# The first attention of a fused transformer kernel: two key/value groups per pass, maxima carried in the queries' fourth slot, one bank for the weighted values of both, and a new order of work

## The chip, the cores and the metric

The kernel runs on one core of one Trainium2 chip. The metric is the time of one execution on the device in microseconds (us), the median of several runs.

## What is computed

The reference is two pre-norm transformer layers on x of 2 batches x 512 tokens x 512 features, in fp32: attention, feed-forward, attention, feed-forward, each added to x. The change touches the first attention. Its heads are small: 32 query heads of 16 features, 8 key/value groups, four query heads to a group.

```python
q, k = _apply_rope(q, cos, sin), _apply_rope(k, cos, sin)
k_h = jnp.repeat(k, GROUP_SIZE, axis=1)          # GROUP_SIZE = 4
scores = jnp.einsum('bhqd,bhkd->bhqk', q, k_h) / math.sqrt(HEAD_DIM)   # HEAD_DIM = 16
attn = jax.nn.softmax(where(causal, min, scores), axis=-1)
ctx = jnp.einsum('bhqk,bhkd->bhqd', attn, v_h)
return ctx.transpose(0, 2, 1, 3).reshape(b, t, D_OUT) @ Wo
```

## The kernel before, in words

TensorE multiplies fp32r operands, so each fp32 value is written as a high part (rounded to fp32r, by ScalarE) and a low part (the rest, by VectorE or GpSimd), and products are summed from such parts. The engines are PE (TensorE), DVE (VectorE), ACT (ScalarE), POOL (GpSimd) and SP (SyncE, which issues the loads).

`project0` (lines 867 to 1008) normalises eight tiles of 128 tokens, turns them, multiplies them with the joined weights and leaves three tensors in SBUF: `q2` and `k2`, four slots of 16 numbers for each head (queries high, low, high, low; keys high, high, low, low, so that 64 rows give all partial products), and `vw`, the values' high and low parts beside a column of ones for the softmax sum. DVE rotates (L984, L989, L990), POOL adds (L1004) and takes the keys' low part (L1007), DVE takes the queries' low part (L959). Before its statistics (L89) DVE sets the ones and zeros of `vw` (L963, L964).

`attend0` (from line 1011) goes over 16 units u, one for each group and batch, the batch changing fastest. A unit has four query tiles i, and tile i meets key tiles 0 to i, so a unit has 10 pairs (i, j), one per tick. The order is written as tables of ticks (`TURN`, `SCORE`, `SHIFT`, `END`, `BACK`) which every engine follows in its own queue. Per unit:

- `turn_qk` (L1117): PE transposes keys, then each query tile, four 64-column transposes at a time, into the one bank `qkbank`; ACT copies them (L1347) to `k_rows` and `q_rows`, which holds four query tiles.
- `scores` (L1129) with the mask (L1132): queries by keys into one of three score banks, 11 banks a unit; DVE takes the negated maxima (L1238).
- `part_maxima` (L1250, L1252) splits the four maxima of a tile into parts, `shift_maxima` (L1165) transposes them through the same `qkbank`, `spread_maxima` (L1260) writes them as eight more rows under the queries.
- `turned_scores` (L1145, mask L1148) computes keys by queries less the maximum, with 72 rows, into one of two banks; ACT takes the exponential (L1353) and its high part (L1359), POOL the low part (L1386).
- `weigh` (L1158, L1159) multiplies high and low parts with `vw`, 33 columns, into `cbank`. DVE reads the bank when a tile i is complete (L1270), `turn_back` (L1175) transposes it per head, and DVE adds the parts and divides by the sums (L1279, L1280, L1286, L1293).

The output projection takes each of eight token tiles when its heads are complete: `turn_tile` (L1203), high part (L1376), low part (L1315), twelve matmuls (`project_tile`, L1216 to L1218), the sum with x (L1329) and the statistics of the next norm (L1331). Because batches alternate, tile 0 comes only in the drain after the last unit and the other seven behind it. The next stage starts when the block has ended on every engine.

## Time and profile before

| | before |
|---|---|
| median of 3 runs | 1594.26 us (1590.72 to 1594.69) |
| profiled execution | 1589.34 us, its span 1587.5 us |
| PE busy, share of the span | 1488.5 us, 94% |
| DVE, ACT, POOL busy | 1080.5, 740.8, 692.0 us |
| mean granted TensorE clock | 0.964 |
| projection stage, from the trace | 0 to 74.5 us |
| first attention with its output projection | 74.5 to 441.0 us |

A matmul is pipelined, so its row is longer than its share of PE; where work follows without a gap, the distance between ends is its cost. PEld is the weight load, which may run beside a matmul. "Issue" is time in which the profile shows nothing that the engine waited for. The clock is in parts of 2.4 GHz; 0.50 is the level of 1.2 GHz.

### The profile page before, as it was taken

The page shows a single profiled execution, that of the slowest core. Times are in us where ns is not written, and L with a number is a line of the kernel's source. Part 1 is how long each engine was busy: PE and PEld are TensorE (multiplying, and loading weights), DVE is VectorE, ACT ScalarE, POOL GpSimd, SP SyncE. Part 2 cuts the span into 40 slices and gives each one's busy share as a digit, 9 for nine tenths or more (in the row PEclk, how much of TensorE's full clock was granted, in tenths as well). Part 3 has the DMA queues.
Part 4 walks back from the last instruction along what each step waited for, and adds up shares of the span by engine and source line. Part 5 has one row for each costly group of instructions (what it writes and reads, how often), then busy time and mean ns, then how long its engine had stood idle before and what let it go on. Part 6 is the DMA issues. An engine that isn't in the chain of part 4 may idle for free. (4 is left out here: it accounts for less than half of the span.)

```text
span 1587.5 us, 21452 instructions
## 1 busy us (share of the span) xinstructions
PE 1488.5 (94%) x7256; PEld 1090.3 (69%) x7256; DVE 1080.5 (68%) x2149; ACT 740.8 (47%) x1590; POOL 692.0 (44%) x528
## 2 busy tenths in 40 slices
PE   4699999999959988999999999999999999789999
PEld 3555555555624446888888888888888888668887
DVE  6678888888574345787777777777787677642322
ACT  3456666666332223445445455454444544443332
POOL 3556666666242324443434434243533334045453
PEclk9879999999869988999999999999999999999999
DMA  2000000000030001100100001010110101023332
GB/s 99 27 1 1 1 1 1 1 1 1 1 100 1 0 24 43 41 28 27 34 21 28 27 27 41 14 40 14 34 34 27 34 1 41 1 74 96 99 97 77
DMA packets 63669, 50.01 MB, mean 32 GB/s; under 512 B 7533, under 2 KB 52973, under 8 KB 63307
## 3 DMA queue, kind: packets, MB, share of 16 engines
q1 hardware_dynamic: 63563, 48.65, 10.5%
q8 instruction: 60, 0.98, 0.3%
q14 instruction: 46, 0.38, 0.1%
HBM read 46.54 MB, written 2.10 MB: 31 GB/s over the span
## 5 line engine op out<-in xcount | busy, mean ns | idle before, releaser
L1386 POOL TENSOR_TENSOR a_p_lo<-a_prob,a_p_hi 128x512 fp32r<-128x512 f32 x160 | 203.5, 1276 | 126.0 <-ACT a_p_hi L1359 124.5
L678 ACT ACTIVATE a_pt_hi<-a_ring 128x512 fp32r<-128x512 f32 x160 | 93.7, 596 | 176.2 <-PE a_ring L388 176.1
L814 POOL TENSOR_TENSOR a_rot_a<-a_rot_a,a_rot_b 128x512 f32<-128x512 f32 x80 | 103.3, 1292 | 148.5 <-DVE a_rot_b L557 147.6
L669 ACT ACTIVATE a_prob<-a_score,a_nmax 128x128 f32<-128x128 f32 (+3 forms) x256 | 131.9, 528 | 57.8 <-DVE a_nmax L522 57.7
L329 PE MATMUL a_xo<-h_hi,a_w_hi 128*128 128x512 f32 x384 | 155.3, 404 | 3.6 <-POOL a_w_lo L824 3.6
L1908 POOL TENSOR_TENSOR f_w_lo<-raw,f_w_hi 128x512 fp32r<-128x512 f32 (+2 forms) x66 | 90.9, 1401 | 142.8 <-ACT f_w_hi L1851 142.7
L331 PE MATMUL a_xo<-h_hi,a_w_lo 128*128 128x512 f32 x384 | 152.0, 396 | 0.0
L330 PE MATMUL a_xo<-h_lo,a_w_hi 128*128 128x512 f32 x384 | 150.9, 393 | 0.0
L1353 ACT ACTIVATE a_prob<-a_turned 128x512 f32<-128x512 f32 x160 | 94.9, 593 | 94.5 <-PE a_turned L1145 53.0
L819 POOL TENSOR_TENSOR a_p_lo<-a_rot_a,a_p_hi 128x512 fp32r<-128x512 f32 x80 | 103.8, 1297 | 72.0 <-ACT a_p_hi L695 72.0
L539 DVE TENSOR_TENSOR a_pt_lo<-a_ring,a_pt_hi 128x512 fp32r<-128x512 f32 x160 | 108.5, 686 | 33.3 <-ACT a_pt_hi L678 32.1
L1238 DVE TENSOR_REDUCE a_nmax<-a_score 128x1 f32<-128x384 f32 (+3 forms) x176 | 109.0, 640 | 30.8 <-PE a_score L1132 30.3
L522 DVE TENSOR_REDUCE a_nmax<-a_score 128x1 f32<-128x384 f32 (+3 forms) x176 | 109.3, 636 | 17.0 <-PE a_score L378 12.0
L824 POOL TENSOR_TENSOR a_w_lo<-raw,a_w_hi 128x512 fp32r<-128x512 f32 x48 | 63.4, 1325 | 105.3 <-ACT a_w_hi L706 104.3
L533 DVE TENSOR_SCALAR a_prob<-a_prob,a_rinv 128x128 f32<-128x128 f32 (+3 forms) x256 | 105.9, 456 | 4.6
L329 PE MATMUL a_xo<-a_wo_hi,a_c_hi 128*128 128x512 f32 x256 | 104.5, 408 | 1.5 <-DVE a_c_lo L544 1.4
L695 ACT ACTIVATE a_p_hi<-a_rot_a 128x512 fp32r<-128x512 f32 x80 | 50.4, 630 | 109.6 <-POOL a_rot_a L814 109.6
L1359 ACT ACTIVATE a_p_hi<-a_prob 128x512 fp32r<-128x512 f32 x160 | 100.3, 627 | 2.7
L331 PE MATMUL a_xo<-a_wo_hi,a_c_lo 128*128 128x512 f32 x256 | 100.3, 392 | 0.0
L330 PE MATMUL a_xo<-a_wo_lo,a_c_hi 128*128 128x512 f32 x256 | 100.1, 391 | 0.0
L329 PE MATMUL a_score<-a_p_hi 128*128 128x128 f32 (+3 forms) x256 | 93.9, 367 | 5.2 <-POOL a_p_lo L819 4.6
L829 POOL TENSOR_TENSOR a_wo_lo<-raw,a_wo_hi 128x512 fp32r<-128x512 f32 x32 | 42.1, 1326 | 124.1 <-ACT a_wo_hi L714 124.1
(273 smaller groups left out, 3938.3 us busy)
## 6 DMA issues: line engine op xcount, KB each, us to landing
raw<-in_L_gate_up_t SPq DMA_DIRECT2D x40, 256.0 KB, 3.0
raw<-in_L_attn_wq SPq DMA_DIRECT2D x32, 256.0 KB, 2.8
raw<-in_L_attn_wo SPq DMA_DIRECT2D x32, 256.0 KB, 2.6
raw<-in_L_down_t SPq DMA_DIRECT2D x20, 256.0 KB, 2.7
x<-in_L_attn_x SPq DMA_DIRECT2D x4, 512.0 KB, 5.2
raw<-in_L_attn_wk SPq DMA_DIRECT2D x8, 256.0 KB, 2.7
raw<-in_L_attn_wv SPq DMA_DIRECT2D x8, 256.0 KB, 2.7
out<-x SPq DMA_DIRECT2D x8, 256.0 KB, 2.5
```

The lines of the kernel that those rows point to most:

```text
L329: nc.tensor.matmul(out, l_hi, r_hi, start=start, stop=False)
L330: nc.tensor.matmul(out, l_hi, r_lo, start=False, stop=False)
L331: return nc.tensor.matmul(out, l_lo, r_hi, start=False, stop=stop)
L522: nc.vector.tensor_reduce(nmax[:, i % 2, bank * per:(bank + 1) * per], score[e % NS][:, 0:per * n].rearrange("p (h n) -> p h n", h=per), A ...
L533: last = nc.vector.tensor_scalar(pr, pr, rinv[:, i % 2, h:h + 1], None, ALU.mult)
L539: nc.vector.tensor_tensor(pt_lo[:, n % NPT, :], ring[n % 2][:, :], pt_hi[:, n % NPT, :].bitcast(F32), ALU.subtract).then_inc(ring_read, 1)
L669: nc.scalar.activation(prob[i % 2][:, h, 0:n], score[e % NS][:, (h % per) * n:(h % per + 1) * n], ACT.Exp, bias=nmax[:, i % 2, h:h + 1], a ...
L814: nc.gpsimd.tensor_tensor(rot_a[:, c % 2, :], rot_a[:, c % 2, :], rot_b[:, c % 2, :], ALU.add).then_inc(summed, 1)
L819: nc.gpsimd.tensor_tensor(p_lo[:, u % 2, c, :], rot_a[:, c % 2, :], p_hi[:, u % 2, c, :].bitcast(F32), ALU.subtract).then_inc(p_ready, 1)
L1238: nc.vector.tensor_reduce(nmax[:, i, bank * per:(bank + 1) * per], score[e % NS][:, 0:per * n].rearrange("p (h n) -> p h n", h=per), AX_X, ...
L1359: nc.scalar.activation(p_hi[:, mm % NP, :], prob[:, mm % NE, :], ACT.Copy).then_inc(p_hi_done, 1)
L1386: nc.gpsimd.tensor_tensor(p_lo[:, mm % NP, :], prob[:, mm % NE, :], p_hi[:, mm % NP, :].bitcast(F32), ALU.subtract).then_inc(p_ready, 1)
```

## The change

A pass now takes a pair of groups of one batch: 8 passes, batch 0 first. Queries and keys of both groups are transposed together with all 128 columns; `k_rows` holds each group's keys with zeros in the other group's 64 rows. The fourth slot of each key is 1 and that of each query 0; once the maxima of a query tile are known, their two parts are put into that slot and the four transposes are done again (`turn_queries` with `again`), and DVE copies the result to `q_max`. The low x low product is left out of the scores. `q_rows` holds one query tile. The weights of both groups give 66 rows of one bank. Tiles, waits and engines follow a new order written out by hand, of which PE's is shown; `first` is the first of two output tiles of batch 0 in the second and third pass of batch 1, `tail` the pass after the last. DVE copies the keys and the second transposes, ACT the first ones. `c_own` is no longer loaded, and the weights' columns are laid out anew on the host.

```diff
     def tokens(self, t):
-        return slice((self.first + t) * P, (self.first + t + 1) * P)
+        at = (self.first + t) % self.wrap
+        return slice(at * P, (at + 1) * P)
...
-                nc.scalar.activation(m.vw[:, t, :, :, 0:HD0], twice(kvbank[t % 2][:, KW:2 * KW]), ACT.Copy).then_inc(read, 1)
+                v = kvbank[t % 2][:, KW:2 * KW].rearrange("p (g x n) -> p g x n", x=2, n=HD0)
+                nc.scalar.activation(m.vw[:, t, :, 1, 0:3:2, 0:HD0], v, ACT.Copy)
+                nc.scalar.activation(m.vw[:, t, :, 0, 0:3:2, 0:HD0], v, ACT.Copy).then_inc(read, 1)
...
-                nc.vector.tensor_tensor(m.q2[:, t, :, 1:4:2, :], twice(rot_a[:, t % 2, 0:QW]),
-                                        m.q2[:, t, :, 0:4:2, :].bitcast(F32), ALU.subtract).then_inc(q_ready, 1)
+                nc.vector.tensor_tensor(m.q2[:, t, :, 1, :], rot_a[:, t % 2, 0:QW].rearrange("p (h n) -> p h n", n=HD0),
+                                        m.q2[:, t, :, 0, :].bitcast(F32), ALU.subtract).then_inc(q_ready, 1)
 
             for t in range(NT):
-                nc.vector.memset(m.vw[:, t, :, :, HD0:HD0 + 1].bitcast(F32), 1.0)
-            nc.vector.memset(m.vw[:, :, :, 1, HD0 + 1:2 * HD0 + 1].bitcast(F32), 0.0).then_inc(v_ready, 1)
+                nc.vector.memset(m.vw[:, t, :, :, 0:3:2, HD0].bitcast(F32), 1.0)
+                nc.vector.memset(m.vw[:, t, :, 1, 0:3:2, HD0 + 1:2 * HD0 + 1].bitcast(F32), 0.0)
+            nc.vector.memset(m.q2[:, :, :, 3, :].bitcast(F32), 0.0).then_inc(v_ready, 1)
             ln.scales(dve)
...
+            nc.gpsimd.memset(m.k2[:, :, :, 3, :].bitcast(F32), 1.0)
+            nc.gpsimd.memset(m.vw[:, :, :, :, 1, :].bitcast(F32), 0.0)
...
-                nc.gpsimd.tensor_tensor(m.k2[:, t, :, 2:4, :], twice(rot_a[:, t % 2, QW:QW + KW]),
-                                        m.k2[:, t, :, 0:2, :].bitcast(F32), ALU.subtract).then_inc(k_ready, 1)
+                nc.gpsimd.tensor_tensor(m.k2[:, t, :, 2, :], rot_a[:, t % 2, QW:QW + KW].rearrange("p (g n) -> p g n", n=HD0),
+                                        m.k2[:, t, :, 0, :].bitcast(F32), ALU.subtract).then_inc(k_ready, 1)
...
+        k_rows = sb("k_rows", [P, 2, X2, T], F32R)
+        q_rows, q_max = sb("q_rows", [P, HPG, P], F32R), sb("q_max", [P, NQ, HPG, P], F32R)
+        nmax = sb("nmax", [P, 2, HPG, X2])
...
+            def claim_qkbank(reader, value):
+
+                if emptied:
+                    pe.wait_ge(*emptied.pop())
+                emptied.append((reader, value))
+
+            def claim_score():
+
+                count["score"] += 1
+                if count["score"] > NS:
+                    pe.wait_ge(score_read, count["score"] - NS)
+                return score[(count["score"] - 1) % NS]
+
...
+            def turn_queries(u, i, again):
+
+                if not live(u):
+                    return
+                b, p, n = u // PAIRS, u % PAIRS, QT * u + i
+                if again:
+                    pe.wait_ge(parted, 2 * (n + 1))
+                    claim_qkbank(qm_read, n + 1)
+                else:
+                    claim_qkbank(q_read, n + 1)
+                for r in range(HPG):
+                    at = X2 * (HPG * p + r)
+                    x = m.q2[:, b * QT + i, at:at + X2, :, :].bitcast(F32)
+                    last = nc.tensor.transpose(qkbank[:, r * P:(r + 1) * P], x.rearrange("p x s n -> p (x s n)"), m.ident[:, :])
+                last.then_inc(qm_turned if again else q_turned, 1)
...
+                if x == 0 and bank == 0:
+                    pe.wait_ge(q_read, QT * u + i + 1)
...
+                    nc.tensor.matmul(out[:, h * n:(h + 1) * n], q_rows[:, bank * per + h, :], k_rows[:, u % 2, x, 0:n],
+                                     start=(h == 0), stop=False)
...
+                last = nc.tensor.matmul(out, k_rows[:, u % 2, x, j * P:(j + 1) * P], q_max[:, (QT * u + i) % NQ, :, :],
...
+                v = m.vw[:, (u // PAIRS) * QT + j, u % PAIRS, :, x:x + 2, :].rearrange("p s c n -> p s (c n)")
+                nc.tensor.matmul(cbank[0:VX, :], v[:, 0, :], p_hi[:, mm % NP, :], start=first, stop=False)
+                nc.tensor.matmul(cbank[0:VX, :], v[:, 1, :], p_lo[:, mm % NP, :], start=False,
+                                 stop=last).then_inc(weighed, 1)
...
+                    last = nc.tensor.transpose(hbank[:, h * VX:(h + 1) * VX], head_t[0:VX, n % 2, h * P:(h + 1) * P],
+                                               m.ident[0:VX, 0:VX])
...
+            for u in range(-1, NU + 1):
+                turn_queries(u - 1, 3, 1)
+                weigh(u - 1, 1, 1, 1)
+                turned_scores(u - 1, 2, 0, 2)
+                turned_scores(u - 1, 2, 1, 2)
+                turn_keys(u)
+                weigh(u - 1, 2, 0, 0)
+                turn_back(u - 1, 1)
+                turned_scores(u - 1, 3, 0, 0)
+                weigh(u - 1, 2, 1, 0)
+                weigh(u - 1, 2, 0, 1)
+                if tail:
+                    turn_tile(QT)
+                scores(u, 0, 0, 0)
+                turn_queries(u, 1, 0)
+                scores(u, 0, 1, 0)
+                weigh(u - 1, 2, 1, 1)
+                turned_scores(u - 1, 3, 1, 0)
+                turned_scores(u - 1, 3, 0, 1)
+                scores(u, 1, 0, 0)
+                weigh(u - 1, 2, 0, 2)
+                weigh(u - 1, 2, 1, 2)
+                turned_scores(u - 1, 3, 1, 1)
+                turn_queries(u, 0, 1)
+                turned_scores(u - 1, 3, 0, 2)
+                if tail:
+                    project_tile(QT)
+                    turn_tile(QT + 1)
+                scores(u, 1, 0, 1)
+                scores(u, 1, 1, 0)
+                scores(u, 1, 1, 1)
+                turn_queries(u, 2, 0)
+                if first is not None:
+                    turn_tile(first)
+                weigh(u - 1, 3, 0, 0)
+                weigh(u - 1, 3, 1, 0)
+                turned_scores(u - 1, 3, 1, 2)
+                scores(u, 2, 0, 0)
+                turned_scores(u - 1, 3, 0, 3)
+                scores(u, 2, 0, 1)
+                scores(u, 2, 0, 2)
+                turn_back(u - 1, 2)
+                scores(u, 2, 0, 3)
+                scores(u, 2, 1, 0)
+                turn_queries(u, 1, 1)
+                weigh(u - 1, 3, 0, 1)
+                turned_scores(u - 1, 3, 1, 3)
+                if tail:
+                    project_tile(QT + 1)
+                turned_scores(u, 0, 0, 0)
+                weigh(u - 1, 3, 1, 1)
+                scores(u, 2, 1, 1)
+                scores(u, 2, 1, 2)
+                turn_queries(u, 3, 0)
+                scores(u, 2, 1, 3)
+                if first is not None:
+                    project_tile(first)
+                    turn_tile(first + 1)
+                weigh(u - 1, 3, 0, 2)
+                turned_scores(u, 0, 1, 0)
+                scores(u, 3, 0, 0)
+                scores(u, 3, 0, 1)
+                scores(u, 3, 0, 2)
+                weigh(u - 1, 3, 1, 2)
+                if tail:
+                    turn_tile(QT + 2)
+                weigh(u - 1, 3, 0, 3)
+                turned_scores(u, 1, 0, 0)
+                scores(u, 3, 0, 3)
+                turned_scores(u, 1, 1, 0)
+                weigh(u - 1, 3, 1, 3)
+                if tail:
+                    project_tile(QT + 2)
+                turn_queries(u, 2, 1)
+                turned_scores(u, 1, 0, 1)
+                scores(u, 3, 1, 0)
+                weigh(u, 0, 0, 0)
+                turn_back(u - 1, 3)
+                scores(u, 3, 1, 1)
+                turned_scores(u, 1, 1, 1)
+                weigh(u, 0, 1, 0)
+                turn_queries(u + 1, 0, 0)
+                turned_scores(u, 2, 0, 0)
+                scores(u, 3, 1, 2)
+                scores(u, 3, 1, 3)
+                if first is not None:
+                    project_tile(first + 1)
+                weigh(u, 1, 0, 0)
+                turned_scores(u, 2, 1, 0)
+                weigh(u, 1, 1, 0)
+                weigh(u, 1, 0, 1)
+                turn_back(u, 0)
+                turned_scores(u, 2, 0, 1)
+                turned_scores(u, 2, 1, 1)
...
+            def put_maxima(u, i):
+
+                if not live(u):
+                    return
+                n, t, at = QT * u + i, (u // PAIRS) * QT + i, X2 * HPG * (u % PAIRS)
+                heads = m.q2[:, t, at:at + X2 * HPG, 3, :]
+                both = nmax[:, i % 2, :, :].rearrange("p h x -> p (h x)")
+                dve.wait_ge(score_read, count["score"])
+                nc.vector.tensor_copy(heads[:, :, 0], both).then_inc(parted, 1)
+                dve.wait_ge(parted, 2 * n + 1)
+                nc.vector.tensor_tensor(heads[:, :, 1], both, heads[:, :, 0].bitcast(F32), ALU.subtract).then_inc(parted, 1)
+
...
+                nc.vector.tensor_copy(k_rows[0:64, u % 2, 0, :], qkbank[0:64, :]).then_inc(keys_read, 1)
+                nc.vector.tensor_copy(k_rows[64:P, u % 2, 1, :], qkbank[64:P, :]).then_inc(keys_read, 1)
+
+            def read_queries(u, i):
...
+                dve.wait_ge(qm_turned, n + 1)
+                if n >= NQ:
+                    s = n - NQ
+                    dve.wait_ge(t_scored, weight_at(s // QT, s % QT, 1, s % QT) + 1)
+                nc.vector.tensor_copy(q_max[:, n % NQ, :, :], qkbank[:, :].rearrange("p (h n) -> p h n", h=HPG)).then_inc(qm_read, 1)
...
+            def read_queries(u, i):
+                if not live(u):
+                    return
+                n = QT * u + i
+                act.wait_ge(q_turned, n + 1)
+                if n >= 1:
+                    act.wait_ge(scored, scored_by(n - 1))
+                nc.scalar.activation(q_rows[:, :, :], qkbank[:, :].rearrange("p (h n) -> p h n", h=HPG),
+                                     ACT.Copy).then_inc(q_read, 1)
...
-                    m.h_hi, m.h_lo = isb("h0_hi", [P, KT, NT * P], F32R), isb("h0_lo", [P, KT, NT * P], F32R)
+                    m.h_hi, m.h_lo = isb("h0_hi", [P, KT, QT * P], F32R), isb("h0_lo", [P, KT, QT * P], F32R)
...
-    out["L0_qkv"] = np.concatenate([a["L0_attn_Wq"], a["L0_attn_Wk"], a["L0_attn_Wv"]], axis=1)
+    wq = a["L0_attn_Wq"].reshape(D, NG // 2, 2, HPG, HD0).transpose(0, 1, 3, 2, 4).reshape(D, -1)
+    out["L0_qkv"] = np.concatenate([wq, a["L0_attn_Wk"], a["L0_attn_Wv"]], axis=1)
```

## Rows read from the trace of the kernel before

**Rows 1.** Busy time by stretch: us, each engine (instructions), clock, DMA share, GB/s
```profile
74.50:88.00 13.50, 12.10 (x42) 6.79 (x42) 5.17 (x12) 3.97 (x6) 0.94 (x1) 0.50 0.24 79
88.00:108.00 20.00, 18.15 (x73) 9.58 (x71) 14.83 (x26) 14.03 (x27) 14.88 (x12) 0.75 0.00 0
128.00:399.00 271.00, 261.08 (x1371) 145.39 (x1370) 230.96 (x589) 189.12 (x340) 174.17 (x138) 1.00 0.00 1
399.00:411.20 12.20, 11.49 (x37) 5.14 (x38) 5.74 (x16) 6.14 (x10) 7.34 (x6) 0.61 0.00 1
411.20:441.00 29.80, 27.14 (x133) 21.66 (x131) 17.25 (x29) 4.69 (x8) 0.00 (x0) 0.99 0.00 1
```

**Rows 2.** Waits of TensorE's weight loads, 239 to 399 us: total, times, longest
```profile
PEld a_turned L1145 <- DVE a_q_rows L1260: 7.9, 8, 1.0
PEld a_qkbank L1165 <- DVE a_split L1252: 6.8, 9, 0.8
```

**Rows 3.** Key transposes: timeline row of one group, then the line's first and last start
```profile
216.88 0.60 PE L1117 MATMUL a_qkbank<-ident,k 128*64 128x128 f32 x4
...
L1117 PE MATMUL a_qkbank<-ident,k x64: 270/272/421, 74.5 to 376.0; 128*64 128x128 f32 x64
```

**Rows 4.** Timeline (start, us, engine, line): transposes at 205, output tiles at 420
```profile
204.87 0.39 PE L1145 MATMUL a_turned<-a_q_rows,a_k_rows 72*128 72x512 f32 x1
205.10 0.60 PE L1117 MATMUL a_qkbank<-ident,q 128*64 128x128 f32 x4
205.63 0.43 PE L1175 MATMUL a_hbank<-ident,a_head_t 33*128 33x33 f32 x4
205.79 0.58 ACT L1347 ACTIVATE a_q_rows<-a_qkbank 64x512 fp32r<-64x512 f32 x1
...
419.95 0.39 PE L1218 MATMUL a_score<-a_wo_hi,a_c_lo 128*128 128x512 f32 x1
420.18 0.60 PE L1203 MATMUL a_turned<-ident,a_head 128*128 128x128 f32 x4
420.51 0.19 PEld L1216 LDWEIGHTS a_score<-a_wo_hi,a_c_hi 128*128 128x128 f32 x1
423.42 0.60 PE L1203 MATMUL a_turned<-ident,a_head 128*128 128x128 f32 x4
```

**Rows 5.** Groups by line and form, 239 to 399 us
```profile
L1386 POOL TENSOR_TENSOR a_p_lo<-a_prob,a_p_hi 128x512 fp32r<-128x512 f32 x82 | 104.3, 1276 | 57.1 <-ACT a_p_hi L1359 56.3
L1359 ACT ACTIVATE a_p_hi<-a_prob 128x512 fp32r<-128x512 f32 x81 | 50.8, 627 | 1.3
L1353 ACT ACTIVATE a_prob<-a_turned 128x512 f32<-128x512 f32 x81 | 48.1, 593 | 46.9 <-PE a_turned L1145 26.4 <-PE a_turned L1148 20.0
L1347 ACT ACTIVATE a_q_rows<-a_qkbank 64x512 fp32r<-64x512 f32 x32 | 18.5, 579 | 0.0
L1270 DVE COPY a_head_t<-a_cbank 33x512 f32<-33x512 f32 x33 | 22.2, 673 | 0.1
L1145 PEld LDWEIGHTS a_turned<-a_q_rows,a_k_rows 72*128 72x128 f32 x81 | 15.7, 194 | 14.9 <-DVE a_q_rows L1260 7.9
L1117 PEld LDWEIGHTS a_qkbank<-ident,q 128*64 128x64 f32 x124 | 13.7, 110 | 4.1
L1165 PEld LDWEIGHTS a_qkbank<-ident,a_split 128*128 128x128 f32 x33 | 4.6, 140 | 9.7 <-DVE a_split L1252 6.8
```

**Rows 6.** Projection stage: timeline rows, then L1004 with its min/median/max ns
```profile
5.47 0.91 DVE L964 MEMSET vw<- 128x1024 f32 x1 [0.15 <-issue]
9.34 2.63 DVE L89 BATCH_NORM_STATS2 stats<-x 128x6 f32<-128x512 f32 x4 [0.24 <-DMA x<-in_L_attn_x]
...
42.16 1.21 DVE L959 TENSOR_TENSOR q<-p_rot_a,q 128x1024 fp32r<-128x1024 f32 x1
...
L1004 POOL TENSOR_TENSOR p_rot_a<-p_rot_a,p_rot_b x8: 1522/2461/2482, 31.4 to 69.4; 128x640 f32<-128x640 f32 x8
```

More of the change, by code:

```diff
@@ L1122, in scores @@
[L1122 to L1127 removed]
+            count = {"score": 0}
+            emptied = []
+            def claim_qkbank(reader, value):
+                if emptied:
+                    pe.wait_ge(*emptied.pop())
+                emptied.append((reader, value))
@@ new lines, in project_tile @@
+                    high = nc.tensor.matmul(out[:, :], c_hi[:, t % 2, k, :], wo_lo[:, k, :], start=False, stop=False)
+                    last = nc.tensor.matmul(out[:, :], c_lo[:, t % 2, k, :], wo_hi[:, k, :], start=False, stop=(k == KT - 1))
+                high.then_inc(projected, 1)
+                last.then_inc(scored, 1)
+            for u in range(-1, NU + 1):
+                first = 2 * (u - PAIRS - 1) if u in (PAIRS + 1, PAIRS + 2) else None
+                tail = u == NU
+                turn_queries(u - 1, 3, 1)
[91 more added lines that the diff above has]
+                turned_scores(u, 2, 1, 1)
@@ L1379, in _ @@
         @block.gpsimd
         def _(pool):
-            nc.gpsimd.memset(k_rows[S64, :, :].bitcast(F32), 1.0).then_inc(ones_set, 1)
-            for mm in range(TICKS * 2 * NG):
+            for mm in range(M_ALL * NU):
                 pool.wait_ge(p_hi_done, mm + 1)
```

492 lines of the change are left out of this document (253 added, 239 removed).

## The prediction

> **What bounds the kernel now.** I read the stretches by stage first, because the change touches only the first projection and the first attention, some 440 of 1587.5 us. In [rows 1] TensorE (PE) is busy in 261.08 of 271.00 us of the attention's even part (96%) at a granted clock of 1.00; VectorE (DVE) has 85%, ScalarE (ACT) 70%, GpSimd (POOL) 64%. So PE sets the pace there, and the question for every edit is what it does to PE's queue. The same rows show where PE is slow for another reason: from 74.50 to 88.00 the clock is 0.50 (the 1.2 GHz level) though PE is busy in 12.10 of 13.50 us, from 88.00 to 108.00 it is 0.75, and from 399.00 to 411.20, where the last weights drain, 0.61.
>
> The second view is what PE waited for in eight units [rows 2]: its weight loads stood 7.9 us for the spread maxima (L1260) and 6.8 us for the split maxima (L1252), the only waits of size on another engine. Part of each lies under a matmul that still runs: PE as a whole idles 9.92 us in the 13.6 units of the even part [rows 1].
>
> The third is the pace. Key transposes of one unit begin at 216.88, and those of the last, eight units on, have their last start at 376.0 [rows 3], some 0.3 us into their group of four: (376.0 - 0.3 - 216.88)/8 = 19.9 us per unit, 39.8 per pair of units. The stage takes 441.0 - 74.5 = 366.5 us. Of these 16 x 19.9 = 318.4 are units; output tiles follow each other at 423.42 - 420.18 = 3.24 us [rows 3, 4], eight are 25.9; the remaining 22.2 are the low clock (half of 24 us at the head, 12; 0.39 of 12.2 us at the drain, 5) and some 5 of filling and draining.
>
> **The change, part by part, per pair of units.** PE's work goes by ends: where work follows without a gap, an instruction costs the distance from the end before to its own.
> - Transposes. Before, a pair has 10 groups of four 64-column ones (keys and queries), 8 single ones of the split maxima and 8 groups of turn-back. After it has 9 groups of four 128-column ones (keys 1, queries 4, queries with maxima 4) and 4 turn-backs of 66 rows. Four of 64 columns end 205.70 (205.10 + 0.60) behind a matmul that ended 205.26: 0.44 us. Four of 128 columns end 420.78 behind 420.34: 0.44. Four turn-backs end 206.06 behind 205.70: 0.36 [rows 4]. A split transpose I put at 0.11, a quarter of the four. Before: 10 x 0.44 + 8 x 0.11 + 8 x 0.36 = 8.2. After: 9 x 0.44 + 4 x 0.40 (the wider output, between 0.36 and 0.44) = 5.6. Removed: 2.6 us.
> - Scores, turned scores, masks and weighings keep their count and free size (22, 20, 8 and 40 per pair). The stationary operand grows in rows (64 or 72 to 128) and for the weighing in columns (33 to 66). The first I cost at nothing: 72 rows load in 0.19 [rows 5] and 128 rows in 0.19 (L1216, [rows 4]). The weighing's load grows only to 66 columns, under that 0.19 of 128, and both lie beneath the 0.23 from one 512-wide matmul's start to the next start (419.95 to 420.18, [rows 4]).
> - Waits removed. The spread from a PSUM slot (L1260) and the split bank go; 9.92 us of idle over 6.8 pairs is 1.5 per pair, the loads' 14.7 over four pairs 3.7. I take 2.2, which is also what 39.8 leaves over the sum of PE's own pieces by ends.
> - Waits added. The queries' buffer is now one instead of four: ACT may copy tile i's queries only when every score of tile i-1 is done, and PE's next scores wait for that copy. This happens four times per pair. In three of them PE has two to four instructions of 0.23 in between, some 0.94 us, and the copy takes 0.58 [rows 5] plus two handovers of about 0.1 (transposes end 205.70, the copy began 205.79, [rows 4]): 0.8. It fits if ACT is free. ACT is a queue of exponentials and high parts of 0.59 and 0.63 us [rows 5], and is 20 x 1.22 + 4 x 0.58 = 26.7 us busy per pair, so it is often in one of them: half of 0.6 late on average. All nine claims of the shared bank (before: 18) and the maxima's second way (a DVE copy as long as L1270's 0.67 [rows 5], with about 2.5 us of PE work in between) add to that. I take 1.7, with bounds 0 and 6.8 (below).
> - Other engines. DVE has 230.96 of 271.00 us [rows 1], 33.9 per 39.8. It loses eight spreads, four head reads and four head takings per pair and gains six copies of 0.67 at most, so it stays below that. POOL keeps 20 x 1.276 = 25.5 [rows 5]. Neither reaches PE's 37.
>
> Sum per pair: -2.6 - 2.2 + 1.7 = -3.1, so 36.7 us, eight of them 293.6, against 318.4.
>
> **Order of the output tiles.** Batch 0 is now complete after half the pairs, and its four tiles go into two middle passes, the other four into the drain. The PE work stays 25.9; it lies beside nothing before and fills gaps of at most a few tenths after. At the drain one chain remains without cover: the last weighing, head read 0.67, turn-back, head taking, tile transposes, high and low part, 2.8 of projection, add and statistics; I add 2 us for it. The stage: 293.6 + 25.9 + 22.2 + 2 = 343.7, or -22.8.
>
> **Projection stage.** DVE now clears the fourth slots of all queries before the statistics: 4096 elements at 0.91 per 1024 [rows 6] is 3.6 us, with eight small memsets about 4.3 less the 0.9 removed. The second four statistics waited only 0.24 us for their data, at 9.34 [rows 6], so DVE has no slack there and nearly all of it, 3.3 us, moves the start of everything. Bounds: 2 (memset faster) and 5. Against it, the low part of the queries halves from 1024 to 512 elements, 1.21 to about 0.68 (a 512-element copy has 0.67). It lies beside POOL's sum of 2.46, whose shortest is 1.52 [rows 6]; a shorter neighbour should give 0.45 back in six tiles, 2.7, and the last low parts end the stage 1 us sooner. ACT's second write of the values is short and fits in its idle time. POOL's new memsets (3136 elements) come while it would wait for the first weights to land. Net -0.4, with bounds -4 and +5. Behind the stage nothing changes.
>
> Sum: -23.2 us. The profiled execution took 1589.34 us (span 1587.5); the median of the three runs is 1594.26, 4.9 above it (0.3%, about what can be told from no change here). On the median: 1571.1, so 1571.
>
> **A rule against it.** The rows give 0.44 for four narrow and for four wide transposes [rows 4]. The Trainium skill ("TensorE: Matmul & The Clock Gate", section "LDWEIGHTS (loading the stationary operand)") says the load time is the number of columns over 1.2 GHz. By it a wide load is 53 ns longer than a narrow one; 36 of them exposed would, as an estimate, take 1.9 us per pair, 15 us in all, from the gain. The same section says that rows don't matter, and there the loads of 72 and 128 rows agree.
>
> **Rivals.**
> 1. The waits vanish (added wait 0): -4.8 per pair, -38.4, with +2 and -0.4: 1557. For it: PE's order keeps work between each producer and consumer. Against: one buffer where there were four. Chance 0.2.
> 2. The wide loads are exposed, or the clock stays low. By rows, 128 columns load in 0.140 and 64 in 0.110 [rows 5]: 36 x 0.03 is 1.1 per pair, 8.6 in all: 1580. The first pass has scores and transposes alone, about 21 us of full-clock work; if the 1.2 GHz level holds through it and through the drain, another 10 to 18 us go: 1581 to 1589. Chance together 0.17. The rule of the Trainium skill above stands beside the first half; by its figure that would be 1586.
> 3. Slower: the copy of the queries becomes the bound. Place: ACT's `read_queries` between two groups of scores. If the exponential queued before it waits for POOL's 1.276 us (three slots of `prob`), each of four copies comes 1.28 + 0.8 + 0.6 after the last score, with 0.94 covered: 1.7, or 6.8 per pair instead of 1.7. Then a pair takes 41.8, +2.0, and the whole +16 - 0.4 + 2: 1612. It decides from an added wait of 4.6 per pair, 1.15 per copy. For it: ACT at 73% in a fixed order. Against: the order puts each copy where its scores should be done. Chance 0.1.
> 4. The change doesn't do what it says, the pace stays 19.9 per unit because PE's modelled work hides a floor elsewhere: 1594 +-4. Chance 0.05.
>
> **Numbers.** The forecast has 0.48; its own range, added waits 0.7 to 2.7 and the start's bounds, is 1562 to 1582. The range takes in rival 1 and most of rival 2: 1550 to 1592. Faster by over 0.3% (below 1589.5): 0.48 + 0.2 + 0.14 = 0.82; same: 0.03 + 0.05 = 0.08; slower: 0.10.
>
> **What would show it.** Key transposes of two units following each other in the even part 36.7 us apart (35 to 38); PE at 96% or more there and its waits now on the copy of queries (ACT) and the second copy (DVE), under 0.3 us each; four wide transposes in 0.44; no L1252 or L1260 left; first statistics near 10 instead of 6.5 us; half clock for about as long at the head. I am wrong if a pair takes over 39.5 us with waits on ACT's copy, if the first pass runs over 35 us, or if the stretch before the first key transposes grows by more than 5 us.

## The result, and the profile after

| | before | after |
|---|---|---|
| median of 4 runs, us | 1592.49 (1588.54 to 1594.69) | 1519.81 (1516.26 to 1523.64) |
| ratio | 1 | 0.9547 [0.9508, 0.9585] |
| profiled execution, us | 1589.34 | 1516.26 |
| its span, us | 1587.5 | 1514.5 |

The change takes 72.7 us off the median. The forecast took off 23 and its range ended at 1550, so the forecast was wrong: right in sign, three times too small.

The first fence is the head of the page of after, busy time and share of each engine over the span. The second is the view of busy time by stretch (columns as in [rows 1]).

```profile
span 1514.5 us, 20230 instructions
...
PE 1411.0 (93%) x7032; PEld 1074.7 (71%) x7032; DVE 1009.6 (67%) x1918; ACT 711.5 (47%) x1550; POOL 689.4 (46%) x529
```

```profile
72.00:90.00 18.00, 14.33 (x59) 10.92 (x58) 11.01 (x20) 3.07 (x4) 0.00 (x0) 0.51 0.19 58
90.00:110.00 20.00, 14.25 (x73) 8.09 (x73) 13.64 (x25) 14.12 (x26) 15.10 (x13) 1.00 0.00 1
130.00:230.00 100.00, 98.75 (x586) 65.48 (x584) 90.25 (x189) 83.18 (x151) 86.74 (x69) 1.00 0.00 1
...
234.00:271.00 37.00, 34.25 (x191) 23.19 (x190) 28.70 (x59) 24.73 (x45) 23.25 (x20) 1.00 0.00 1
360.00:371.00 11.00, 7.62 (x34) 5.35 (x34) 4.97 (x11) 0.60 (x1) 0.00 (x0) 1.00 0.00 0
```

In the even part PE is busy 98.75 of 100 us, where [rows 1] has 261.08 of 271.00. The shares, 98.75% and 96%, hardly differ, yet the pace does. A group of key transposes now opens a pass over two units (timeline rows: start, duration, engine, line):

```profile
73.54 1.11 PE L1106 MATMUL a_qkbank<-ident,k 128*128 128x128 f32 x4 [0.69 <-ACT a_q_rows L1468]
...
140.76 0.66 PE L1106 MATMUL a_qkbank<-ident,k 128*128 128x128 f32 x4
...
170.29 0.66 PE L1106 MATMUL a_qkbank<-ident,k 128*128 128x128 f32 x4
...
229.40 0.66 PE L1106 MATMUL a_qkbank<-ident,k 128*128 128x128 f32 x4
```

A pair of units takes (229.40 - 140.76)/3 = 29.55 us (29.6 below), against 39.8 before [rows 3] and 36.7 in the forecast. All eight passes begin at 73.54, 109.89, 140.76, 170.29, 199.84, 229.4, 268.65 and 308.18: the first takes 36.35 (half clock up to 90, some 16 us of it), the two that carry two output tiles each 39.2 and 39.5.

What held PE back in the even part, first the weight loads and then PE as a whole (columns as in [rows 2], 130 to 230 us):

```profile
PEld a_score L1140 <- issue: 7.3, 35, 0.3
PEld a_turned L1156 <- issue: 5.6, 24, 0.3
PEld a_qkbank L1122 <- DVE q L1334: 2.9, 4, 0.7
PEld a_qkbank L1106 <- DVE a_q_max L1356: 0.8, 4, 0.2
PEld a_score L1137 <- ACT a_q_rows L1468: 0.8, 3, 0.3
```

```profile
PE a_qkbank L1122 <- DVE q L1334: 1.2, 4, 0.3
```

The waits for the split and spread maxima, 14.7 us in four pairs in [rows 2], are gone. In their place stands 1.2 us in 3.4 pairs, at the second transposition of the queries (L1122, for the low part of the maxima, L1334). The copy of the queries (L1468), the centre of the forecast's added waits, delays loads by 0.8 us in all.

The first attention stage now runs from 71.7 to 371.6, 299.9 us against 366.5; the stage before it ends 2.8 earlier. In the projection stage (timeline rows):

```profile
6.73 3.47 DVE L968 MEMSET q<- 128x4096 f32 x1 [0.80 <-issue]
10.12 4.78 DVE L89 BATCH_NORM_STATS2 stats<-x 128x6 f32<-128x512 f32 x8
```

and, by line and form, 20 to 74 us:

```profile
L1010 POOL TENSOR_TENSOR p_rot_a<-p_rot_a,p_rot_b 128x640 f32<-128x640 f32 x8 | 15.5, 1935 | 13.4 <-DVE p_rot_b L994 13.4
...
L962 DVE TENSOR_TENSOR q<-p_rot_a,q 128x512 fp32r<-128x512 f32 x8 | 5.7, 715 | 2.8 <-ACT k L933 2.8
```

### The profile page after: what moved, and what is told of

Read it like the earlier page. It is cut to its first block and busy times, and to the rows that moved or that the text cites. A ratio compares the mean times of both kernels' runs of the same rounds, so it can differ in the third digit from the quotient of the medians.

```text
span 1514.5 us, 20230 instructions
## 1 busy us (share of the span) xinstructions
PE 1411.0 (93%) x7032; PEld 1074.7 (71%) x7032; DVE 1009.6 (67%) x1918; ACT 711.5 (47%) x1550; POOL 689.4 (46%) x529
## 5 line engine op out<-in xcount | busy, mean ns | idle before, releaser
L523 DVE TENSOR_REDUCE a_nmax<-a_score 128x1 f32<-128x384 f32 (+3 forms) x176 | 109.3, 636 | 17.3 <-PE a_score L379 12.2
L1320 DVE TENSOR_REDUCE a_nmax<-a_score 128x1 f32<-128x512 f32 (+3 forms) x176 | 105.1, 635 | 20.2 <-PE a_score L1140 20.1
L534 DVE TENSOR_SCALAR a_prob<-a_prob,a_rinv 128x128 f32<-128x128 f32 (+3 forms) x256 | 99.2, 430 | 4.5
```

The lines of the kernel that those rows point to most:

```text
L523: nc.vector.tensor_reduce(nmax[:, i % 2, bank * per:(bank + 1) * per], score[e % NS][:, 0:per * n].rearrange("p (h n) -> p h n", h=per), A ...
L534: last = nc.vector.tensor_scalar(pr, pr, rinv[:, i % 2, h:h + 1], None, ALU.mult)
L1320: nc.vector.tensor_reduce(nmax[:, i % 2, bank * per:(bank + 1) * per, x], next_score()[:, 0:per * n].rearrange("p (h n) -> p h n", h=per), ...
```

## The experiments

A pair is 7.1 us shorter than forecast, and added waits that did not come are only 1.3 of it. The rest lies in what I took for PE's own work, or in waits that the kernel before had. Two theories stood against each other. **R, rows:** a stationary operand of 64 rows among operands of 128 costs something that does not show as the duration of its load. **O, order:** the old order with the maxima's way through DVE (split, transposed, spread) has a floor of its own, which my 2.2 us of removed waits undercounted. I began from before and made its operands full one after another, then went back from after. Times with their before are medians measured on the same chip; "pace" is the distance between key transposes in the trace, per unit (before 19.9) or per pair.

**Control.** Before, with the keys copied into two slots by the same ACT instruction (one for each kind of scores), and two buffers sharing space to make room.

```diff
-        k_rows = sb("k_rows", [P, B, T], F32R)
+        k_rows = sb("k_rows", [P, B, 2, T], F32R)
```

> Control for the next kernel: the kernel before, with the keys copied by ACT into two slots of k_rows at once (one write of 1024 instead of 512 elements per unit) and the output weights kept in the not yet used half of head. All products and their row counts are as before. Every theory: the unit keeps its 19.9 us within 0.2, the whole is within 5 us of the kernel before.

Measured: 1601.08, one run, 14 above the median of before on that chip and 2.2 above the slowest of its 15 runs (1579.39 to 1598.86), so the expected 5 us were missed. The trace shows one place: from 90 to 126 us the clock was 0.50 to 0.58, where before had 0.78 to 0.91 in the same stretch. In the even part the pace is 20.12 against 19.85, so the control brings nothing by itself; 0.3 us per unit are lost.

**Scores over 72 rows** instead of 64, eight of them zero in the keys' slot; the products are the same.

```diff
-                    nc.tensor.matmul(out[:, h * n:(h + 1) * n], q_rows[0:64, i, bank * per + h, :],
-                                     k_rows[0:64, u % 2, 0, 0:n], start=(h == 0), stop=False)
+                    nc.tensor.matmul(out[:, h * n:(h + 1) * n], q_rows[0:S64.stop, i, bank * per + h, :],
+                                     k_rows[0:S64.stop, u % 2, 0, 0:n], start=(h == 0), stop=False)
```

> The control with one edit: the scores' matmuls contract over 72 rows (eight of them zero) instead of 64. Theory R (rows: a stationary operand of at most 64 rows between operands of 128 rows is not loaded under the matmul before it, so each score and each mask behind it pays its load in the open): a score bank of 512 with its mask falls from 0.57 to about 0.36 us, as after the change; 11 banks give 2.0 to 2.5 us per unit, 16 units 32 to 40 us, so about 1552 to 1562 us, less if another engine's wait comes up. Rival O (order: the loss was waits that the old order of ticks forced, and rows cost nothing): a unit stays at 19.9 and the whole at 1590 +- 5.

Measured: 1575.04 against 1587.07, 0.9926 [0.9892, 0.9959]; pace 19.13. Its timeline at one full-width score, and what its loads waited for from 130 to 330 us:

```profile
213.42 0.19 PEld L1131 LDWEIGHTS a_score<-a_k_rows,a_q_rows 72*128 72x128 f32 x1
213.45 0.48 PE L1131 MATMUL a_score<-a_k_rows,a_q_rows 72*128 72x512 f32 x1
213.77 0.10 PEld L1134 LDWEIGHTS a_score<-mask_b,ident_b 128*128 128x128 bf16 x1 [0.15 <-issue]
```

```profile
PEld a_qkbank L1167 <- DVE a_split L1254: 15.9, 32, 1.0
PEld a_turned L1147 <- DVE a_q_rows L1262: 14.4, 21, 0.8
```

Two scores of full width in a row, with the mask between them, first here and then in before, where they have 64 rows:

```profile
228.34 0.51 PE L1131 MATMUL a_score<-a_k_rows,a_q_rows 72*128 72x512 f32 x1
228.69 0.23 PE L1134 MATMUL a_score<-mask_b,ident_b 128*128 128x128 bf16 x1
228.73 0.48 PE L1131 MATMUL a_score<-a_k_rows,a_q_rows 72*128 72x512 f32 x1
```

```profile
212.78 0.48 PE L1129 MATMUL a_score<-a_k_rows,a_q_rows 64*128 64x512 f32 x1
213.19 0.23 PE L1132 MATMUL a_score<-mask_b,ident_b 128*128 128x128 bf16 x1
213.35 0.18 PEld L1129 LDWEIGHTS a_score<-a_k_rows,a_q_rows 64*128 64x128 f32 x1
213.35 0.50 PE L1129 MATMUL a_score<-a_k_rows,a_q_rows 64*128 64x512 f32 x1
```

The second score begins 0.39 us behind the first, in before 0.57. The difference has two parts: from a score's start to its mask's are 0.32 to 0.35 us instead of 0.41, and from the mask's start to the next score's 0.04 instead of 0.16. So both loads come late in before, that of the 64-row score and that of the 128-row mask behind it. More rows for PE, and it is faster: R is at work. But a unit gave only 1.0 of the 2 to 2.5 that 11 banks at 0.2 promise, and the time lies above the expected 1552 to 1562. The view of waits in the control has 9.3 and 8.2 for the split and the spread maxima, where this one has 15.9 and 14.4. What PE saved, it mostly waited for the maxima.

**And the turn-back over 66 rows** (33 of them zero), on top of the last:

```diff
-                    last = nc.tensor.transpose(hbank[:, h * VW:(h + 1) * VW], head_t[0:VW, n % 2, h * P:(h + 1) * P],
-                                               m.ident[0:VW, 0:VW])
+                    last = nc.tensor.transpose(hbank[:, h * VB:(h + 1) * VB], head_t[0:VB, n % 2, h * P:(h + 1) * P],
+                                               m.ident[0:VB, 0:VB])
```

> The kernel before with scores of 72 rows and turn-backs of 66 rows instead of 33 (the added rows are zeros). Theory R: four turn-backs fall from 0.36 to about 0.25 us and what stands behind them loads early again, so 0.4 to 0.8 us per unit below the kernel with scores of 72 rows alone, 6 to 13 us in all. Rival O: no difference from the kernel before, or slightly longer for the wider output.

Measured: 1573.11, 0.9922 [0.9897, 0.9947]; pace 19.13. By ends, four turn-backs fall from the 0.36 of [rows 4] to 0.25, and the unit does not become shorter, where 0.4 to 0.8 us were expected.

**And everything wide**: the weighing with 66 columns instead of 33, key and query transposes with 128 instead of 64 (the neighbour's columns go along, unused).

```diff
-                nc.tensor.matmul(cbank[0:VW, :], v[:, 0, :], p_hi[:, mm % NP, :], start=(j == 0), stop=False)
+                nc.tensor.matmul(cbank[0:2 * VW, :], m.vw_flat[:, at:at + 2 * VW], p_hi[:, mm % NP, :], start=(j == 0), stop=False)
...
-                        x = m.q2[:, b * QT + s - 1, HPG * g + r, :, :]
+                        x = m.q2_all[:, b * QT + s - 1, HPG * g + r:HPG * g + r + 2, :, :]
```

> The kernel before with nothing below 65 rows or columns on the array: scores of 72 rows, turn-backs of 66, weighings of 66 columns and transposes of queries and keys of 128 columns (the extra columns are a neighbour's and not read). Order, passes and engines stay. Theory R alone: what remains to the new kernel is 2.6 us of transposes per pair, so a unit of about 16 to 17 us and the whole near 1535 to 1545. Theory R with O (both count): the unit stops at 17.3 to 18 us with waits on the maxima's way. Rival O alone: 1590 +- 5.

Measured: 1568.72, 0.9902 [0.9867, 0.9937]; pace 19.13 a third time. Waits of its loads, and its row of busy time by stretch:

```profile
PEld a_qkbank L1172 <- DVE a_split L1259: 17.3, 21, 1.2
PEld a_turned L1152 <- DVE a_q_rows L1267: 16.0, 21, 1.0
```

```profile
130.00:330.00 200.00, 178.39 (x1056) 112.92 (x1056) 180.09 (x449) 149.77 (x262) 132.92 (x106) 1.00 0.00 1
```

Three kernels with different work for PE and one pace: in the old order something other than PE's work holds the unit at 19.13. I had expected 16 to 18 with R, with or without O.

What columns cost can't be read from this pace, since something else holds it; the ends show it. Weighings with 66 columns follow each other 0.23 us apart in after (starts 188.45, 188.68, 188.91), those with 33 columns 0.24 in before (214.66, 214.90). Four transposes of 128 columns end 0.43 behind the matmul before them (after with 64-row turned scores: 199.79 and 199.36), four of 64 columns 0.44 [rows 4]. PE's busy time in 200 us is 178.39 here and 177.60 in the kernel before this one. So columns cost next to nothing, neither 33 to 66 nor 64 to 128, which answers the first half of rival 2. By the Trainium skill ("TensorE: Matmul & The Clock Gate", section "LDWEIGHTS (loading the stationary operand)") each load grows with its columns; the load rows do, from 110 to 140 ns for 64 and 128 columns [rows 5], by 30 ns and not by the 53 that the page's rule gives as an estimate. The distances between ends don't grow.

**The other way round: after, with scores over 64 rows.** Each group's scores contract only its own half of the rows; the other half is zero, so the sums are the same.

```diff
-                    nc.tensor.matmul(out[:, h * n:(h + 1) * n], q_rows[:, bank * per + h, :], k_rows[:, u % 2, x, 0:n],
+                    nc.tensor.matmul(out[:, h * n:(h + 1) * n], q_rows[64 * x:64 * x + 64, bank * per + h, :], k_rows[64 * x:64 * x + 64, u % 2, x, 0:n],
```

> The changed kernel with the scores contracted over the 64 rows of their own group (0 to 63 or 64 to 127) instead of over 128, half of which are zero: the same sums. Theory R (a stationary operand of 64 rows beside one of 128 loads in the open): 22 banks and their masks lose about what b1 won, 0.1 to 0.2 us each, so a pair of groups goes from 29.6 to 32 to 34 us and the whole by 20 to 35 us, to 1540 to 1555. Rival O (rows cost nothing): 29.6 and 1520 +- 5; two row halves might even run beside each other and save a little.

Measured: 1562.73 against 1588.91, 0.9859 [0.9815, 0.9904]; pairs begin at 151.63, 186.88 and 222.08, 35.2 apart: +5.6 per pair of 22 banks, 0.25 each, more than the expected 0.1 to 0.2 (a pair of 32 to 34, 1540 to 1555 in all). Timeline of this kernel:

```profile
198.45 0.40 PE L1153 MATMUL a_turned<-a_q_max,a_k_rows 128*128 128x512 f32 x1
198.78 0.18 PEld L1137 LDWEIGHTS a_score<-a_k_rows,a_q_rows 64*128 64x128 f32 x1 [0.36 <-issue]
198.78 0.44 PE L1137 MATMUL a_score<-a_k_rows,a_q_rows 64*128 64x384 f32 x1
199.15 0.10 PEld L1140 LDWEIGHTS a_score<-mask_b,ident_b 128*128 128x128 bf16 x1 [0.18 <-issue]
199.15 0.23 PE L1140 MATMUL a_score<-mask_b,ident_b 128*128 128x128 bf16 x1
```

and of after, scores of full width:

```profile
187.46 0.48 PE L1137 MATMUL a_score<-a_k_rows,a_q_rows 128*128 128x512 f32 x1
...
187.78 0.10 PEld L1140 LDWEIGHTS a_score<-mask_b,ident_b 128*128 128x128 bf16 x1 [0.15 <-issue]
187.78 0.23 PE L1140 MATMUL a_score<-mask_b,ident_b 128*128 128x128 bf16 x1
187.79 0.20 PEld L1137 LDWEIGHTS a_score<-a_k_rows,a_q_rows 128*128 128x128 f32 x1
187.82 0.48 PE L1137 MATMUL a_score<-a_k_rows,a_q_rows 128*128 128x512 f32 x1
```

In after the next score's load begins at 187.79, 0.22 us before the mask's row ends (188.01), and bank follows bank in 187.82 - 187.46 = 0.36 us. With 64 rows the load begins at 198.78, only 0.07 before the row of the turned score ahead of it ends (198.85), after 0.36 us of idle. The mask behind shows the same: its load begins 0.07 before the end of the 64-row score (199.15 and 199.22), but 0.16 before that of the 128-row score (187.78 and 187.94). The loads' own durations are alike, 0.18 and 0.20: not the load is dearer, its place is.

**After, with turned scores over 64 rows**, the same edit at the other product:

```diff
-                last = nc.tensor.matmul(out, k_rows[:, u % 2, x, j * P:(j + 1) * P], q_max[:, (QT * u + i) % NQ, :, :],
+                last = nc.tensor.matmul(out, k_rows[64 * x:64 * x + 64, u % 2, x, j * P:(j + 1) * P], q_max[64 * x:64 * x + 64, (QT * u + i) % NQ, :, :],
```

> The changed kernel with the turned scores (20 matmuls of 512 columns per pair) contracted over the 64 rows of their own group instead of 128: the same sums. Theory R: each stands between operands of 128 rows, so about 0.15 to 0.2 us per matmul and as much for what follows: a pair goes from 29.6 to 32 to 34 us, the whole to 1540 to 1555. Rival O: 29.6 and 1520 +- 5.

Measured: 1548.5, 0.9763 [0.9729, 0.9796]; pair 33.83, +4.3 for 20 matmuls, 0.21 each. One of them, in the timeline:

```profile
197.75 0.50 PE L1137 MATMUL a_score<-a_k_rows,a_q_rows 128*128 128x512 f32 x1
...
198.09 0.23 PE L1140 MATMUL a_score<-mask_b,ident_b 128*128 128x128 bf16 x1
198.24 0.18 PEld L1153 LDWEIGHTS a_turned<-a_q_max,a_k_rows 64*128 64x128 f32 x1
198.25 0.50 PE L1153 MATMUL a_turned<-a_q_max,a_k_rows 64*128 64x512 f32 x1
```

The matmul before it is the mask, whose row ends at 198.32; the load begins 0.08 before that, where the 128-row load above began 0.22 before the end of such a mask. Before had 72 rows here [rows 4], so this price was never paid before the change; it is a second measurement of the same effect.

**What holds the old order at 19.13.** From the all-wide kernel, the spread of the maxima writes one head's columns instead of four:

```diff
-                nc.vector.tensor_tensor(q_rows[S64, i, :, :],
+                nc.vector.tensor_tensor(q_rows[S64, i, 0:1, :],
```

> The kernel before with nothing below 65 rows or columns (unit 19.13 us), and the spread of the maxima writes one head's columns instead of four; it leaves out the maxima of three heads. Theory D (what held the unit at 19.13 in three kernels with different PE work is DVE's queue with the maxima's way in it: split, transpose, spread): 4 spreads shorter by about 0.4 us, unit 17.4 to 18.2. Rival P (PE's own instructions are the 19.13): unit stays at 19.1.

Measured: 1557.48 (one run), pace 18.08, 1.05 less, in the band of the theory that DVE's queue with the maxima's way in it holds the unit.

The same, and the head read copies 128 of 512 columns:

```diff
-                nc.vector.tensor_copy(head_t[0:VW, n % 2, :], cbank[0:VW, :])
+                nc.vector.tensor_copy(head_t[0:VW, n % 2, 0:P], cbank[0:VW, 0:P])
```

> The same, and the copy of the weighted values reads 128 of 512 columns; it leaves out the maxima and the results of three heads of four. Theory D with the whole queue as the bound: another 0.27 to 0.4 us for each of 4 copies, unit down to 16.9 to 17.3, where PE's own work ends it. Theory D with only the maxima's way as the bound: no further fall. Rival P: 19.1.

Measured: 1545.62 (one run), pace 17.70, only 0.38 less, between the two bands expected. DVE's busy time fell by 1.2 and then 1.3 us per unit (from the stretch rows), so its total alone is not the bound; the length of the maxima's way was the better candidate. The next one tests it.

**The all-wide kernel without the maxima's way.** The maxima are taken and not used: no split, no transposed split, no spread, and PE waits for none of them.

```diff
-    SHIFT = {6: (1, 0), 8: (1, 1), 9: (1, 2), 3: (0, 3)}
+    SHIFT = {}
...
-                if j == 0:
-                    pe.wait_ge(max_rows, QT * u + i + 1)
```

> The kernel before with nothing below 65 rows or columns (unit 19.13 us) and the maxima taken but not used: no split, no transpose of the split, no spread, so the exponentials are taken without subtracting the maximum and nothing on PE waits for DVE's maxima. PE loses 4 single transposes per unit, 0.45 us. If the maxima's way through DVE is what held that kernel: the unit falls to what PE's own work is, 15.5 to 16.5 us. If other waits of the old order (bank of the weighted values, copies by ACT) hold as much: 17 to 18.5. If PE's instructions themselves are the 19.13: 18.7.

Measured: 1521.75 (one run). Key transposes, and the busy row:

```profile
220.94 0.60 PE L1122 MATMUL a_qkbank<-ident,k 128*128 128x128 f32 x4
...
236.91 0.60 PE L1122 MATMUL a_qkbank<-ident,k 128*128 128x128 f32 x4
```

```profile
130.00:330.00 200.00, 194.62 (x1222) 133.69 (x1221) 168.97 (x390) 174.70 (x314) 159.66 (x126) 1.00 0.00 1
```

The pace is 15.97, in the band that says the maxima's way held it: 19.13 - 15.97 = 3.2 us per unit. Four split transposes at 0.11 are work left out; the other 2.7, 5.4 per pair, was waiting, direct or behind it. This takes away DVE's splits and spreads together with the waits (DVE is busy 3.7 us less per unit, and PE's wait for its head read is gone too, 6.1 us in 200 in the all-wide kernel), so it shows what the way costs as a whole, not which link of it.

This kernel's pair of 31.9 us can be compared with after's 29.6, since neither has 64-row operands nor the long way. One more group of transposes and four more turn-backs make 0.44 + 4 x 0.25 = 1.4 of the difference, the idle time that is left (5.4 us in 200 here, 1.25 in 100 there) 0.5; 0.5 is unassigned.

**After once more**, as the partner of the next two:

> The changed kernel once more, on the chip of the next two: 1520 +- 5 us, a ratio of 0.955 to the kernel before.

Measured: 1518.61 against 1589.16, 0.9555 [0.9527, 0.9583]. Its seventh pass begins at 265.56 where the first trace has 268.65, and yet both stages end at 371.6. The 3.1 us are lost in the drain, where the clock was 0.79 from 352 to 360 us and 0.75 from 366 to 372; in the first trace it was 1.00 from 308 us on. Behind the stage the code is the same in every kernel here, and that part took between 1139 and 1148 us in the fourteen traces.

**After, with the fourth slots of the queries cleared by POOL** instead of DVE:

```diff
-            nc.vector.memset(m.q2[:, :, :, 3, :].bitcast(F32), 0.0).then_inc(v_ready, 1)
...
             nc.gpsimd.memset(m.vw[:, :, :, :, 1, :].bitcast(F32), 0.0)
+            nc.gpsimd.memset(m.q2[:, :, :, 3, :].bitcast(F32), 0.0)
```

> The changed kernel with the zeros of the queries' fourth slots (4096 elements per partition) written by POOL, idle then, instead of DVE ahead of its statistics. If the 3.47 us memset delays everything behind it: statistics begin near 6.5 instead of 10.1 us and end near 12 instead of 14.9, and the first key transposes come 2 to 3 us earlier, the whole 2 to 3 us shorter. Rival (the start is paced by the weights' parts on POOL, which now also has the memset): 0 +- 1.

Measured: 1518.18, 0.9557 [0.953, 0.9583], the same as after. In the trace the first key transposes come at 70.79 instead of 73.29, 2.5 sooner, POOL taking 3.52 us for it. The stage ends at 370.0, only 1.6 sooner: the second pass took 30.81 us against 29.25, with a clock of 0.54 to 0.61 from 106 to 110 us. The median shows 0.4 of it. That is the rival's 0 +- 1, but not for the rival's reason, since the start did move.

**And the first output tile's transposes two weighings and a turned score later** in PE's order:

```diff
-                if first is not None:
-                    turn_tile(first)
                 weigh(u - 1, 3, 0, 0)
                 weigh(u - 1, 3, 1, 0)
                 turned_scores(u - 1, 3, 1, 2)
+                if first is not None:
+                    turn_tile(first)
```

> The same, and in the two passes with output tiles of batch 0 the first tile's transposes come three steps later, behind two weighings and a turned score, so that they no longer wait for ACT's copy of the queries right before them. If that wait (0.8 us, twice) is what makes these passes 39.2 instead of 29.6 + 6.5 us: each 0.8 to 1.5 us shorter, 2 to 3 in all. Rival (the loss is the shared bank, held by the tile until its low part is read): 0 to 0.5 each.

Measured: 1514.04 (1513.21 to 1515.97), 0.9529 [0.9505, 0.9554]: the lowest time of all, 4.6 under after on the same chip (1518.61), though the two ratios' intervals overlap. The passes with tiles take 38.3 and 38.6 instead of 39.3 and 39.6, 2.0 us together, in the expected band; the rest of the 4.6 is not shown to come from this edit.

## Why the prediction was wrong

**The step that failed** is in the change part by part: "The stationary operand grows in rows (64 or 72 to 128) ... The first I cost at nothing: 72 rows load in 0.19 [rows 5] and 128 rows in 0.19 (L1216, [rows 4])." Both durations are right, and beside the point. A score's 64-row load begins only about 0.07 us before the matmul ahead of it ends, a 72- or 128-row one 0.2 and more before, and the mask's load behind a 64-row score is late as well. The price was in the trace: two scores of full width of before begin 0.57 us apart (212.78 and 213.35, mask between them, shown above), which I took for what a score and its mask cost, and carried over. After has 0.36. With 64 rows put back, after loses 5.6 us per pair. I had also compared only 72 with 128 rows; the one form that mattered, 64, was missing from the comparison. And I had allowed this step no gain, so the range had nothing for it.

The Trainium skill ("TensorE: Matmul & The Clock Gate", section "LDWEIGHTS (loading the stationary operand)") says rows don't matter, and for a load's duration the trace agrees (0.18 to 0.20 us). The same page, section "Step-by-step: what each phase is for", has a condition that I passed over: loads are pulled ahead of running matmuls "when (a) the row groups don't conflict, or (b) the LDWEIGHTS targets the background weight buffer". The runs show that the loads of 64-row operands between taller ones come late here, and do not show which of the two conditions fails, nor why 72 rows are enough.

**The second step, "Waits removed ... I take 2.2",** was right for the kernel as it was and too small for the kernel as it became. In before the waits lay largely behind PE's own work (3.7 us of load waits per pair, 1.5 of idle; my 2.2 was a choice between them). When that shrinks and the order stays, the waits grow: the unit stops at 19.13 in three kernels, giving 2.0 per pair of the 5.6 (from the control), and 5.4 come only when the maxima's way goes. That is about the 2.2 together with the 3.6 that the waits had swallowed. So neither half explains the result alone. The padding alone brings 0.7 to 1.0%, the change 4.5%, and the change with its scores back at 64 rows 1.4%.

**The sum per pair,** corrected: 39.8, less 5.6 for rows of the scores, less 2.6 for transposes as forecast, less 0.6 for the turn-back's rows (four groups at 0.25 instead of 0.40), less the 2.2 of waits, plus 0.4 of idle that is left (1.25 us in 3.4 pairs), is 29.2; measured 29.6. The forecast was 36.7; between them are 7.1, of which these terms make 7.5: 5.6 + 0.6 for rows, 1.7 - 0.4 = 1.3 for added waits that did not come; 0.4 is unassigned.

**Added waits,** 1.7 with bounds 0 and 6.8: measured 0.4, near the lower bound. ACT is in time with its copy of the queries. As to waits rival 1 was right, but its 1557 carried the same wrong price of the scores.

**The rest of the stage** was mis-sized the other way. Outside 8 x 29.6 and eight tiles of 3.24 (25.9) the forecast had 22.2 + 2 = 24.2; measured is 299.9 - 236.8 - 25.9 = 37.2. The parts, from the starts of the passes: head 8.6 (clock 0.51 for some 18 us, 12 forecast), the second pass 1.3, two passes with tiles 2 x 3.3, and 20.8 behind the last full pass. There the forecast had 12, 5 of it for the low clock; in this trace the clock is 1.00 from 308 us on, so filling and draining alone took 20.8 where 7 were forecast. "It lies beside nothing before and fills gaps" was wrong for the tiles: once the gaps are gone, they interrupt. PE's waits from 234 to 308, and from 308 to 372 us:

```profile
PE a_qkbank L1191 <- ACT a_q_rows L1468: 1.6, 2, 0.8
PE a_score L1201 <- DVE a_nmax L1320: 1.3, 2, 0.7
PE a_qkbank L1122 <- DVE a_c_lo L1387: 1.0, 4, 0.3
```

```profile
PE a_score L1201 <- DVE a_c_lo L1387: 4.2, 3, 1.9
PE a_qkbank L1122 <- DVE q L1334: 1.5, 1, 1.5
PE a_qkbank L1191 <- DVE a_head L1383: 1.1, 1, 1.1
```

A tile's transposes (L1191) wait for the shared bank, which ACT's copy still holds (L1468, 0.8 each time). That moving them later takes 1.0 off each such pass fits this; it does not show that the bank is the only cause. In the drain the projection waits for the low part of each tile (L1387): the chain without cover, larger than my 2.

**The projection stage** gave 2.8 instead of 0.4. The memset took 3.47 (forecast 3.6), but the first tile's rotation came only 1.8 later (31.46, before 29.70); I had passed on 3.3. The statistics, one block of 4.78 us with their data there, ended 2.9 later than before (14.90 and 11.97); where the other 1.1 went is not shown. The tiles then follow each other at 5.02 instead of 5.41 us (31.46 to 56.58 and 29.70 to 56.76, five steps each), 0.4 a tile as forecast (0.45), with POOL's sum at 1.94 instead of a mean of 2.15.

**The totals.** Forecast -22.8 for the stage: eight pairs of 7.1 more are -56.8, the rest +13.0, together -66.6, which is the measured difference because the rest was taken as what is left. With -2.8 for the projection stage that is -69.4 of the span's -73.0. The remaining 3.6 us lie behind the stage, where the change does nothing and the fourteen traces differ by up to 8.

**Other rivals.** 2: columns were free by ends, and the half clock at the head was shorter, not longer, though the first pass exceeded my limit of 35 us by 1.35 (by 0.08 in the second trace of after). 3: the copy never became the bound, no L1468 wait over 0.8. 4: refuted. Of my signs the ones on waits, transposes (four in 0.44) and L1252, L1260 held; "36.7 us apart (35 to 38)" failed below.

**PE's share of busy time** misled, too. Before was 96% busy at 39.8 us a pair, after 98.75% at 29.6, with 22 scores, 20 turned scores and 40 weighings in both. A matmul row lasts 0.39 to 0.50 us where its successor may follow after 0.23, so a stall of 0.2 before a load hides under the row of the matmul before. The Trainium skill ("Perfetto Trace Analysis", section "Identifying the Most-Contended Engine") warns of this and names two measures instead, one of them the busy share of the weight loads. Here that share was 145.39 of 271.00 (54%, [rows 1]) and is 65.48 of 100, so the trace agrees in direction: it rises 1.2 times, the pace 1.35 times.

## What to carry to other kernels

Price PE's instructions by the distance from end to end, each form apart, and look for forms with few rows: here a product over 64 rows between products over 128 cost 0.21 to 0.25 us more than one padded with zeros to 128, and a score with its mask 0.18 more than one padded to 72. When PE's own work shrinks, ask which chain through other engines was just long enough to be hidden; the padding alone gave 2.0 us per pair, the padding without the maxima's way 8.3 (20.12 to 15.97 per unit). And where an edit is costed at nothing, let the range hold a gain as well as a loss.

## What the runs showed of the hardware

- A load of 64 rows between taller operands began 0.07 to 0.08 us before the row of the matmul ahead of it ended (198.24 under the mask that ran to 198.32; 198.78 and 198.85), loads of 72 and 128 rows 0.2 us and more before (213.42 under the transposes that ran to 213.69; 187.79 under the mask that ran to 188.01). 72 rows were enough for the effect; the turn-back fell from 0.36 (33 rows) to 0.25 (66 rows) for four.
- The bf16 mask's load behind a score began 0.07 before that score's row ended when it had 64 rows, 0.16 before when it had 128.
- Moving the stationary operands from 33 to 66 and from 64 to 128 columns lengthened their loads by 0.03 us and the distances between ends not at all (0.24 and 0.23 per weighing, 0.44 and 0.43 for four transposes).
- Before a bf16 mask, the weight loads stood 0.15 to 0.3 us for nothing that the profile shows, in after too (7.3 us in 35 of them per 100 us), while the score's matmul ran. It is not explained; no run tried it.
- Clearing 4096 fp32 elements per partition took 3.47 us on DVE and 3.52 on POOL.
